# Macaron block: mixture layers grouped by expert over DRAM slots, slot tiles turned by a transposing DMA

## The reference

```python
x = x + 0.5 * ffn(layernorm(x))
x = x + attn(layernorm(x))
x = x + 0.5 * ffn(layernorm(x))

# ffn, for every row h (E = 4 experts, H = 512):
g = softmax(layer_norm(h) @ router_w.T)
top2_w, top2_idx = top_k(g, 2); top2_w /= sum(top2_w) + 1e-8
hid = relu(layer_norm(h @ w1[e], ln_g[e], ln_b[e]))      # for all e
expert_out = hid @ w2[e]                                  # for all e
out = layer_norm(sum over the two chosen e of top2_w * expert_out[e])

# attn: 16 heads of 16, linear attention with a causal running sum
Z_cum = cumsum(V outer K); Y = Q . Z_cum; return Y @ Wo.T + bo
```

## Time and profile before

| | |
|---|---|
| three runs, median (lowest to highest) | 1240.5 us (1240.02 to 1240.84) |
| profiled execution, span of its core | 1236.4 us, 25066 instructions |
| busy: PE, DVE, POOL, ACT | 1140.2, 948.3, 672.0, 512.8 us |
| TensorE clock granted, mean | 0.978 of full speed |
| DMA traffic | 20.69 MB, mean 17 GB/s |

### The profile page before, as it was taken

The page is one execution under the profiler, slowest core; times in us unless marked ns, Lnnn a source line. Parts: engine busy times, 40 slices in busy tenths (PEclk is TensorE's granted clock), DMA queues, the critical chain, the costliest instruction groups (busy, mean ns, idle before and its releaser), DMA issues.

```text
span 1236.4 us, 25066 instructions
## 1 busy us (share of the span) xinstructions
PE 1140.2 (92%) x8694; PEld 731.9 (59%) x8694; DVE 948.3 (77%) x2150; ACT 512.8 (41%) x878; POOL 672.0 (54%) x1039
## 2 busy tenths in 40 slices
PE   4669799999999999889999999889999999999996
PEld 4335456656566566656666666556566665666664
DVE  5678787887978878657777777578879787797875
ACT  4353324233342424456665666442333424334131
POOL 2365546454565544498778777543555654546360
PEclk9789989999999999999999999899999999999998
DMA  9002000000000000000000000000000000000000
GB/s 286 4 1 69 1 1 2 1 2 1 0 0 0 1 2 1 19 18 15 11 13 18 17 18 18 1 2 2 17 1 18 1 19 18 0 17 1 19 18 17
DMA packets 29037, 20.69 MB, mean 17 GB/s; under 512 B 7812, under 2 KB 27784, under 8 KB 28808
## 3 DMA queue, kind: packets, MB, share of 16 engines
q1 hardware_dynamic: 24112, 18.36, 5.4%
q10 hardware_dynamic: 4824, 1.07, 0.5%
HBM read 11.03 MB, written 4.19 MB: 12 GB/s over the span
## 4 chain that ended last, share of the span: by engine, by line
PE 48%; DVE 19%; issue 16%; POOL 10%; ACT 4%; DMA 2%; DVEq 1%; ACTq 0%; POOLq 0%
PE bank L1547 7%; PE bank L1549 6%; PE bank L1548 6%; DVE area L674 5%; DVE area L682 4%; PE bank L1532 4%; PE bank L1534 4%; PE bank L1533 4%; DVE area L655 4%; PE bank L1506 4%; POOL area L487 3%; PE bank L1555 2%; PE bank L1557 2%; PE bank L1556 2%; DMA betas<-in_L_ffn_ln_b_dram 2%
## 5 line engine op out<-in xcount | busy, mean ns | idle before, releaser
L1256 ACT ACTIVATE area<-area 128x512 f16<-128x512 f32 x256 | 160.9, 630 | 387.9 <-DVE area L674 386.1
L1547 PE MATMUL bank<-w2h,area 128*128 128x256 f16 x1024 | 281.3, 275 | 12.9 <-DVE area L693 7.2
L1548 PE MATMUL bank<-w2l,area 128*128 128x256 f16 x1024 | 280.5, 274 | 0.0
L1549 PE MATMUL bank<-w2h,area 128*128 128x256 f16 x1024 | 280.5, 274 | 0.0
L674 DVE SCALAR_TENSOR_TENSOR area<-area,betas,bank 128x512 f32<-128x512 f32 x256 | 189.9, 743 | 46.0 <-PE bank L1534 37.6
L682 DVE SCALAR_TENSOR_TENSOR area<-area 128x512 f16<-128x512 f32 x256 | 188.7, 737 | 20.3 <-ACT area L1256 17.1
L1532 PE MATMUL bank<-hTh,w1h 128*128 128x512 f16 x512 | 195.5, 382 | 6.7 <-DVE area L674 6.7
L1533 PE MATMUL bank<-hTl,w1h 128*128 128x512 f16 x512 | 195.1, 381 | 0.0
L1534 PE MATMUL bank<-hTh,w1l 128*128 128x512 f16 x512 | 194.9, 381 | 0.0
L696 DVE SCALAR_TENSOR_TENSOR area<-bank,coef,area 128x256 f32<-128x256 f32 x192 | 92.1, 482 | 79.3 <-PE bank L1549 78.1
L487 POOL TENSOR_TENSOR area<-area 128x512 f16<-128x512 f32 x96 | 119.9, 1274 | 45.1 <-ACT area L1300 44.9
(11 more groups left out here) (233 smaller groups left out, 2109.6 us busy)
## 6 DMA issues: line engine op xcount, KB each, us to landing
X<-in_L_attn_x_dram SPq DMA_DIRECT2D x8, 512.0 KB, 7.1
area<-area SPq DMA_DIRECT2D x128, 32.0 KB, 2.0
out_dram<-X SPq DMA_DIRECT2D x7, 512.0 KB, 2.9
area<-in_L_ffn_w_dram SPq DMA_DIRECT2D x4, 512.0 KB, 9.9
X<-in_L_ffn_w_dram SPq DMA_DIRECT2D x2, 1024.0 KB, 15.7
area<-in_L_ffn_ln_g_dram ACTq DMA_DIRECT2D x1, 1024.0 KB, 6.1
out_dram<-X SPq DMA_DIRECT2D x4, 128.0 KB, 1.7
area<-in_L_attn_Wq_dram SPq DMA_DIRECT2D x1, 256.0 KB, 9.2
```

Of the source, the lines that this page charges most:

```text
L1256: act.activation(Rh[:, e % 2, m, :], V[:, a % NV], ACT.Relu).then_inc(s_Rh, 1)
L1547: pe.matmul(dst, Rh[:, e % 2, k, rows], w2h[:, e, k, :], start=(k == 0), stop=False)
L1548: pe.matmul(dst, Rh[:, e % 2, k, rows], w2l[:, e, k, :], start=False, stop=False)
L1549: last = pe.matmul(dst, Rl[:, e % 2, k, rows], w2h[:, e, k, :], start=False, stop=(k == HC - 1))
```

## The change

The mixture layer is rewritten. A group is 16 tiles (2048 rows); a mixture layer has two groups. For each group:

1. `rows`, `row_low`: each tile is normalized into `hrow`, 256 high and 256 low float16 values per row. TensorE transposes it in float16 (`rows_T`) for the router alone.
2. `logits`, `choose`, `positions`, `gates` on DVE, `prefix` on TensorE: for every row its two experts and, by a prefix count, a slot number for each. Slots are ordered by expert, each expert's part rounded up to tiles of 128, so a group has at most NJ = 35 slot tiles, and 35 are always computed (70 per mixture layer, 140 in the kernel).
3. `scatter(G)`: 32 indirect DMAs on GpSimd write the rows to their slots in DRAM (1 KB per row).
4. For each slot tile S: SP loads it as rows (`load_slots`) and once more through a transposing DMA (`load_slots_T`, one instruction, 128 x 512 float16 from DRAM). TensorE reads the tile's expert number into a register (`expert`) and picks the weights with it. gram, layer 1 (now with the weights moving side swapped: 24 matmuls of 128 columns), layer 2 (12 of 256). The bias enters as a row of w1. GpSimd makes the two powers of one tile's variance (`slot_std`). SP stores the result (128 KB) to DRAM.
5. `gather`: two indirect DMAs per tile of rows fetch its two results; ACT and DVE add them with the gates, normalize and add to X.

The routing of the second group stands in slots 2 to 21 of the first, its `scatter` behind slot 21; the first group's `gather` stands in slots 38 to 53; the second group's gathers follow the last slot. The weaving with the attention is gone: `attention` starts with a wait for all 32 tiles of x, computes its own weights, and the second mixture layer starts on each engine behind the attention. All loops are written out, so that there are no hardware loops. All clears of the slot memory (4.6 MB per group buffer) are DMAs in the first stage.

```diff
+    slots_in = [nc.dram_tensor(f"slots_in{b}", (NJ * P, 2 * D), F16).ap() for b in range(2)]
+    slots_out = [nc.dram_tensor(f"slots_out{b}", (NJ * P, D), F32).ap() for b in range(2)]
...
+            def load_slots(S):
+                G, J = group(S)
+                if J == 0:
+                    sp.wait_ge(sc_h[G % 2], 16 * 2 * GT * (G // 2 + 1))
+                if S < R_HS:
+                    sp.wait_ge(zeroed[0], 16)
+                wait(sp, b_h2, S - R_HS + 1)
+                sp.dma_start(hs[:, S % R_HS].rearrange("p c d -> p (c d)"),
+                             slots_in[G % 2][J * P:(J + 1) * P, :]).then_inc(l_hs[S % R_HS], 16)
+            def load_slots_T(S):
+                G, J = group(S)
+                wait(sp, b_A, S - R_HT + 1)
+                sp.dma_start_transpose(hT[:, S % R_HT], slots_in[G % 2][J * P:(J + 1) * P, :]
+                                       ).then_inc(l_hT[S % R_HT], 16)
+            def store_slots(S):
+                G, J = group(S)
+                sp.wait_ge(b_Y, S + 1)
+                if J == 0 and G >= 2:
+                    sp.wait_ge(c_acc, GT * (G - 1))
+                sp.dma_start(slots_out[G % 2][J * P:(J + 1) * P, :], ysb[:, S % R_Y]).then_inc(st_y[S % R_Y], 16)
...
+            def scatter(G):
+                pool.wait_ge(r_pos, G + 1)
+                pool.wait_ge(r_hl, GT * (G + 1))
+                if G < 2:
+                    pool.wait_ge(zeroed[G], 16)
+                else:
+                    pool.wait_ge(b_h2, NJ * (G - 1))
+                for t in range(GT):
+                    for k in range(2):
+                        pool.indirect_dma_start(slots_in[G % 2],
+                                                bass.IndirectOffsetOnAxis(pos[:, G % 2, k, t:t + 1], 0),
+                                                hrow[:, t].rearrange("p c d -> p (c d)"), None
+                                                ).then_inc(sc_h[G % 2], 16)
...
+            def slot_std(S):
+                pool.wait_ge(b_ve, S + 1)
+                wait(pool, b_Y, S - 3)
+                k = S % 4
+                pool.tensor_tensor(stds[:, k], vare[:, k:k + 1].to_broadcast([P, 2]), expo[:, :],
+                                   ALU.pow).then_inc(b_sd, 1)
...
+            def gather(i):
+                G, t = i // GT, i % GT
+                if t == 0:
+                    for r in range(R_Y):
+                        pool.wait_ge(st_y[r], 16 * uses(NJ * (G + 1), r, R_Y))
+                wait(pool, c_acc, i - R_C + 1)
+                for k, d in enumerate((yA, yB)):
+                    pool.indirect_dma_start(d[:, i % R_C], None, slots_out[G % 2],
+                                            bass.IndirectOffsetOnAxis(pos[:, G % 2, k, t:t + 1], 0)
+                                            ).then_inc(g_y[i % R_C], 16)
...
+                for s in range(SF):
+                    t = s + 2 - A_AT
+                    if 0 <= t < GT and t % TB == 0:
+                        quad_rstd(GQ * (G + 1) + t // TB)
+                    if s + 2 < SF:
+                        slot_std(S0 + s + 2)
...
+                        add_offset(GT * (G + 1) + t)
+                    if s == CHAIN_AT + 1:
+                        scatter(G + 1)
...
+                    t = s - C_AT - 2
+                    if 0 <= t < GT:
+                        token_rstd(GT * G + t)
+                    t = s - C_AT
+                    if 0 <= t < GT:
+                        gather(GT * G + t)
+                for t in range(GT + 1):
+                    if t < GT:
+                        gather(GT * (G + 1) + t)
+                    if t >= 1:
+                        token_rstd(GT * (G + 1) + t - 1)
...
+            def rows(i):
+                Q, t = i // TB, i % GT
+                b, k = Q % GQ, i % TB
+                act.wait_ge(r_nr, Q + 1)
+                wait(act, r_hl, i - TB + 1)
+                act.activation(h[:, k, :], X[:, i % NT, :], ACT.Identity,
+                               bias=xnr[:, b, k:k + 1], scale=xrs[:, b, k:k + 1])
+                G = i // GT
+                if t == 0 and G >= 1:
+                    act.wait_ge(sc_h[(G - 1) % 2], 16 * 2 * GT * ((G - 1) // 2 + 1))
+                act.activation(hrow[:, t, 0], X[:, i % NT, :], ACT.Identity,
+                               bias=xnr[:, b, k:k + 1], scale=xrs[:, b, k:k + 1]).then_inc(r_hh, 1)
...
+            def token_sum(i):
+                r, b = i % R_C, i % 2
+                G = i // GT
+                dve.wait_ge(c_ya, i + 1)
+                dve.wait_ge(r_gate, G + 1)
+                dve.scalar_tensor_tensor(out=acc[:, r], in0=yB[:, r], scalar=gate[:, G % 2, 1, i % GT:i % GT + 1],
+                                         in1=acc[:, r], op0=ALU.mult, op1=ALU.add).then_inc(c_acc, 1)
+                dve.wait_ge(c_acc, i + 1)
+                step(dve.bn_stats(ast[:, b, :], acc[:, r]))
+                wait(dve, c_rs, i - 1)
+                step(dve.bn_aggr(amv[:, b, :], ast[:, b, :]))
+                dve.tensor_scalar(ave[:, b:b + 1], amv[:, b, 1:2], EPS, None, ALU.add).then_inc(c_mv, 1)
...
-            def layer1(n, par, e, m):
-                for c in range(KC):
-                    pe.matmul(o, w1h[:, e, c, cols], hTh[:, par, c, :], start=(c == 0), stop=False)
-                    pe.matmul(o, w1h[:, e, c, cols], hTl[:, par, c, :], start=False, stop=False)
-                    last = pe.matmul(o, w1l[:, e, c, cols], hTh[:, par, c, :], start=False, stop=(c == KC - 1))
...
+            def expert(S):
+                G, J = group(S)
+                if J == 0:
+                    pe.wait_ge(r_tab, G + 1)
+                return pe.value_load(etab[0:1, G % 2, J:J + 1], min_val=0, max_val=E - 1)
...
+            def layer1(S, e):
+                pe.wait_ge(b_sdr, S + 1)
+                wait(pe, b_Rl, S - 1)
+                if S == 0:
+                    pe.wait_ge(p_w1l, E)
+                a = hT[:, S % R_HT]
+                for m in range(HC):
+                    o = bank[S % 2][:, m * P:(m + 1) * P]
+                    cols = slice(m * P, (m + 1) * P)
+                    for c in range(KC):
+                        pe.matmul(o, w1h[:, bass.ds(e, 1), c, cols], a[:, c], start=(c == 0), stop=False)
+                        pe.matmul(o, w1h[:, bass.ds(e, 1), c, cols], a[:, KC + c], start=False, stop=False)
+                        last = pe.matmul(o, w1l[:, bass.ds(e, 1), c, cols], a[:, c], start=False, stop=(c == KC - 1))
+                last.then_inc(b_A, 1)
...
+                for S in range(S0, S1):
+                    s = S - S0
+                    t = s - A_AT
+                    if 1 <= t <= GT:
+                        rows_T(GT * (G + 1) + t - 1)
+                    if S + 2 < S1:
+                        e[S + 2] = expert(S + 2)
+                        gram(S + 2, e[S + 2])
+                    layer1(S, e[S])
+                    if 1 <= t <= GT:
+                        router(GT * (G + 1) + t - 1)
+                    if S + 1 < S1:
+                        std_T(S + 1)
+                    if s >= 1:
```

1887 lines of the change are left out of this document (864 added, 1023 removed).

## The result

| | before | after |
|---|---|---|
| runs, median (lowest to highest) | 1240.67 us (1240.02 to 1241.47) | 1454.97 us (1452.71 to 1458.51) |
| profiled span | 1236.4 us | 1453.9 us |
| busy PE, DVE, POOL, ACT | 1140.2, 948.3, 672.0, 512.8 us | 946.8, 793.1, 716.4, 485.9 us |

What follows compares the result with a forecast made beforehand. TensorE's columns were taken to bound the kernel in both mixture layers. First layer 187 + 318 + 61 = 566, attention 325, second layer 104 + 318 + 61, last store 2: span 1376, forecast 1380 us, range 1250 to 1610.

Steps and rivals of the forecast that it cites:

- A: The forecast case: empty starts, middles and tails take more than the columns give back; 1290 to 1480 us, chance 0.57.
- B: Rival: the transposing DMA sets the slot, from 3.8 us per transpose on; 1688 us at 6 us; chance 0.15.
- C: Rival: scatters and gathers are dearer, each holding GpSimd's queue 2.2 us; 1540 us; chance 0.13.
- D: Rival: an indirect DMA hardly holds GpSimd's queue, deciding below 0.34 us each; 1220 us at 0.2; chance 0.13.
- x: Time one indirect DMA of 128 rows holds GpSimd's queue, taken as 1.2 us; the sum moves 160 us per us.
- the slot, 3.8 us: Each of 140 slots on TensorE: 3.17 us of columns, 0.45 for the expert's load, 0.2 for semaphore waits.
- Router 9 us and DVE 6 us: Additions per body: router matmuls in slots 2 to 17, 9 us; DVE over TensorE in slots 38 to 53, 6 us.
- Scatter hole 33 + 4: Mid-body: slot 24's power waits behind 32 scatters, 33 us; the choice's chain costs 4 more.
- Starts: Time before the first slot's layer 1: 187 us in the first layer, 104 in the second with TensorE idle.
- Tail: Second group's gathers after the last slot: 3.5 us per tile, 56 for 16 and 5 to start, 61 us.
- Attention: Eight blocks of 35.0 us, 280, plus 40 us formerly hidden in front and 5 to fill: 325 us.
- Hidden costs: Transposing DMA (issue 0.4 to 1 us, behind four slots of lead) and the clears, both priced at nothing.

Runs made afterwards that it cites:

- plain_row_load: Changed kernel with the slot's transposing DMA replaced by a plain DMA of the same 128 KB, tile left unturned: 1452.05 us, ratio 1.1722.
- spread_scatter: Changed kernel with the second group's 32 scatters issued over eleven slots, two or four a slot, instead of one block: 1388.52 us, ratio 1.1204.
- both_static: Changed kernel with scatters spread over slots, GpSimd work in the starts reordered, and fixed expert addresses for all three products: 1277.64 us, ratio 1.0295.

## Why the prediction was right, and where its sum was not

- *Columns and rivals.* Right. The quiet slot without register instructions takes 3.40 us; the forecast had 3.17 of columns and 0.2 of waits. A was the case that came. B is out by plain_row_load. C and D are out by the cadence of the scatters, 1.27 us, where x was taken as 1.2.
- *The term that was mis-sized is the slot, 3.8 us.* It measured 4.57, and 0.77 x 140 = 108 us is more than the whole miss of 78; other terms give the rest back, as the next points show. The step that failed is "one before every second matmul of 0.055 us just hides". It priced a register instruction at its own 0.032 us and compared it to the matmul beside it. The runs showed that an instruction adds about 0.1 us to a sequencer's sum, that the load adds 0.63, and that what counts is this sum over the whole slot against TensorE's 3.40 us. With the load, 0.45 was taken as a cost in itself; a load costs nothing with fixed addresses, and one more adds 0.63 in this kernel.
- *Router 9 us and DVE 6 us.* With fixed addresses the router's slots take 0.55 more than quiet ones, as forecast, and the DVE-bound ones 4.18 (forecast 4.4, which is 0.6 over 3.8 and not the 0.4 that the 6 us were worked out with). Under a sequencer that needs 4.57 most of it is covered: the router's slots take 4.7, the others 4.57. That gives back 13 us per layer. A body by these figures: 70 x 0.77 = 54, less 13, plus 4 for its hole (next point), is 45 us over the forecast; 43.5 and 42.5 were measured.
- *Scatter hole 33 + 4.* It measured 38.6 (52.3 less 13.7), and 2.8 for the choice's chain, 41 in all. spread_scatter shows that the hole is the block's and not the scatters'. In the body (403 to 478 us), beside DVE's work, an indirect DMA takes 1.02 us in the median and 1.12 at most, against 0.96 in the tail, so nothing of the dearer kind that rival C allowed for appears.
- *Starts.* 187 and 104 against 185.5 and 95.5. The first scatter starts at 109.7 (forecast 110). In the second start it comes 40.7 us behind the attention, where 50 were forecast, and that is all of the 8.5 us. The additions to X take 0.72 us each, not 0.86.
- *Tail.* 3.5 us a tile forecast, 3.47 measured (the gate's product on ACT, L1144, from 552.55 to 604.64 us in 15 steps). The second tail is 7 us over: the last addition to X ends 62.75 us behind the body, and from there to the end of the span are 7.15 us, where 2 were forecast for the last store. *Attention.* 320 against 325.
- *Hidden costs.* The transposing DMA at nothing: right. Its issue, estimated at 0.4 to 1 us, is 1.2.
- *Slips of arithmetic, which did not decide.* D's border by the stated slope is x = 0.325, not 0.34; 1610 us is a transpose of 5.4 us, not 5.3; 33 + 8.9 is 42, not 44.

What stays open: how the sequencer's 4.57 us divide. Only the slopes of the gram's four instructions and of the load were measured. If all 28 cost 0.11 us, they and the load make 3.7 us (an estimate from these two slopes) and leave 0.9 for the 42 matmuls. Also open is whether a kernel that follows the routing can do with fewer of them, by fetching the expert's weights to a fixed place, say. That was not tried.

## What to carry to other kernels

When a loop takes its operands at addresses in registers, add up the sequencer's work over a whole pass of the loop (in this kernel about 0.1 us for each register instruction and 0.6 for a load into a register with its followers), and compare it with the engine's own work; instructions that hide in one kernel cost their full price in another. Where the sequencer was the longer here, the instructions taken away helped wherever they stood; where it was the shorter, a load more or less changed nothing. Columns saved on the busiest engine pay only if it is kept busy: TensorE was idle for 507 us of the span (1453.9 less 946.8), 355 of them in starts and tails, against 96 before, when the neighbouring layer's work filled the borders.

## What the runs showed that I had not expected

- An indirect DMA of 128 rows holds GpSimd's queue for 1.27 us (0.96 busy, 0.30 to the next), for rows of 1 KB.
- The transposing DMA of 128 x 512 float16 takes 1.2 us of SP's queue, a plain one of the same size 0.32, with no difference in the kernel's time.
- A load into a register shows 0.30 us in its row and adds, with its two followers, 0 or 0.63 us, by which sum is the longer.
- Four more transposes on TensorE added 0.15 us to a slot bound by the sequencer; 0.04 us for each, an estimate that has the two added semaphore waits in it, and less than half of what a register instruction adds.
- Spreading the scatters uncovered a border that the block had hidden: rows that go through DRAM can't be loaded before the last scatter has landed, 3.8 us of waiting in spread_scatter and 4.9 in both_static.
- The granted clock was 0.50 to 0.63 of full speed in the starts and tails (0.50 is the lower of the two levels, 1.2 GHz). It also fell to 0.50 in the hole of the first body (0.50 from 310 to 334 us, with TensorE idle) and stayed there at its end: the first layer 2 behind the hole has its matmuls of 256 columns 0.21 us apart (334.60 to 334.82) in place of 0.11, which costs about 1.2 us for its 12 (an estimate from these starts). From 338 us on it is 1.00 (2.4 GHz), with TensorE busy for 52.12 of the 55 us from 344 to 399. Two rows of the same form as the table of stages:

```profile
334.00:336.00 2.00, 1.89 (x10) 1.24 (x11) 1.90 (x9) 0.00 (x0) 0.70 (x1) 0.50 0.03 8
338.00:340.00 2.00, 1.99 (x23) 1.38 (x23) 0.65 (x3) 0.56 (x2) 0.70 (x1) 1.00 0.20 66
```
